# Layer norm's weight and bias folded into three evictions, its centring moved to GpSimd, and softmax sums taken over two banks at a time

## What is computed

```python
def layer0(z, ln_w, ln_b, Wq, Wk, Wv, Wg, bg, Wo, bo):      # H = 8 heads, C = 16
    mu = jnp.mean(z, axis=-1, keepdims=True)
    var = jnp.var(z, axis=-1, keepdims=True)
    zn = (z - mu) * jax.lax.rsqrt(var + EPS) * ln_w + ln_b
    q, k, v = zn @ Wq, zn @ Wk, zn @ Wv                     # each reshaped to heads
    g = jax.nn.sigmoid(zn @ Wg + bg)
    att = jnp.einsum('iabhc,jabhc->ijabh', q, k) * (1.0 / np.sqrt(C))
    att = jax.nn.softmax(att, axis=1)                       # over the 16 sequences j
    o = jnp.einsum('ijabh,jabhc->iabhc', att, v) * g
    return o.reshape(n, l, l, H * C) @ Wo + bo
x = x + layer0(_gn(x), ...)      # _gn: each sequence and channel normalised over the 32 x 32 positions
x = x + layer1(_gn(x), ...)
```

## Time and profile before

| | us |
|---|---|
| median of 3 runs (lowest, highest) | 340.28 (339.03, 341.97) |
| the profiled execution's own time | 342.18 |
| its span, first to last instruction | 340.2 |
| DVE / PE / ACT / POOL busy | 250.9 / 247.4 / 215.8 / 196.5 |
| first layer's strips, periods 0 to 9 | about 37 to 260 of the span |

### The profile page before, as it was taken

The page is one execution under the profiler, slowest core; times in us unless marked ns, Lnnn a source line. Parts: engine busy times, 40 slices in busy tenths (PEclk is TensorE's granted clock), DMA queues, the critical chain, the costliest instruction groups (busy, mean ns, idle before and its releaser), DMA issues.

```text
span 340.2 us, 7453 instructions
## 1 busy us (share of the span) xinstructions
PE 247.4 (73%) x2978; PEld 145.4 (43%) x2982; DVE 250.9 (74%) x463; ACT 215.8 (63%) x392; POOL 196.5 (58%) x172
## 2 busy tenths in 40 slices
...
DMA packets 34893, 19.66 MB, mean 58 GB/s; under 512 B 21228, under 2 KB 31788, under 8 KB 34860
## 3 DMA queue, kind: packets, MB, share of 16 engines
...
## 4 chain that ended last, share of the span: by engine, by line
DVE 40%; PE 40%; ACT 11%; issue 6%; DMA 1%; DVEq 0%; POOL 0%
PE PS L1128 35%; DVE nmax L899 5%; DVE t_sb L883 5%; DVE S_sb L903 5%; DVE og L876 4%; DVE gn_part L966 3%; DVE sums L827 3%; ACT PP L631 2%; PE PS L1197 2%; DVE Z L1115 2%; PE PS L1393 2%; DVE rden L845 1%; ACT t_sb L615 1%; DVE Z L1119 1%; ACT S_sb L621 1%
## 5 line engine op out<-in xcount | busy, mean ns | idle before, releaser
L1128 PE MATMUL PS<-znT,A_bd 128*128 128x512 f16 x192 | 47.0, 386 | 11.3 <-DVE t_sb L883 10.1
L428 POOL TENSOR_TENSOR S_sb<-S_sb,rden 128x512 f32<-128x512 f32 x32 | 35.5, 1133 | 27.6 <-DVE rden L845 27.6
L883 DVE TENSOR_TENSOR t_sb<-PS,t_sb 128x512 f16<-128x512 f32 x64 | 41.2, 684 | 9.2 <-ACT t_sb L615 8.7
L615 ACT CAST t_sb<-PS 128x512 f16<-128x512 f32 x64 | 36.6, 618 | 13.8 <-PE PS L1128 12.5
L621 ACT ACTIVATE S_sb<-S_sb 128x512 f32<-128x512 f32 x32 | 20.3, 634 | 31.7 <-DVE S_sb L903 31.7
L434 POOL TENSOR_TENSOR PP<-S_sb,PP 128x512 f16<-128x512 f32 x28 | 31.8, 1158 | 9.5 <-ACT PP L609 9.5
L1128 PE MATMUL PS<-zbd,t_sb 128*128 128x64 f16 x768 | 27.7, 196 | 12.9 <-DVE t_sb L883 12.2
L1128 PEld LDWEIGHTS PS<-zbd,t_sb 128*128 128x128 f16 x768 | 24.9, 100 | 24.0 <-DVE t_sb L883 16.5
L1128 PEld LDWEIGHTS PS<-znT,A_bd 128*128 128x128 f16 x192 | 16.7, 98 | 39.9 <-DVE t_sb L883 23.8
L411 POOL TENSOR_TENSOR ln_rs<-ln_ve,minus_half 128x16 f32<-128x16 f32 x7 | 20.4, 2914 | 23.0 <-DVE ln_ve L822 23.0
L601 ACT COPY u_sb<-PS 128x512 f32<-128x512 f32 x64 | 33.1, 642 | 0.2 <-PE PS L1128 0.2
...
## 6 DMA issues: line engine op xcount, KB each, us to landing
...
th<-k_dram SPq DMA_DIRECT2D x16, 128.0 KB, 2.7
...
PP<-u_sb SPq DMA_DIRECT2D x8, 128.0 KB, 2.4
```

The costliest lines, as they stand in the source:

```text
L428: nc.gpsimd.tensor_tensor(P, P, bcast(rden[:, 32 * k:32 * k + 32], 2, N), ALU.mult).then_inc(p_nrm, 1)
L615: nc.scalar.copy(t_sb[:, HI, :, h], bank_tg(h)[:, :].rearrange("p (q i) -> p q i", i=N)).then_inc(t_hi, 1)
L883: nc.vector.tensor_tensor(t_sb[:, LO, :, h], bank_tg(h)[:, :].rearrange("p (q i) -> p q i", i=N), t_sb[:, HI, :, h], ALU.subtract).then_in ...
L1128: return nc.tensor.matmul(o, l, r, start=start, stop=stop)
```

## The change

- ln_w and ln_b leave the stream of tokens. `pool_ln_back` loses its last two products, and strip 0 its two on DVE. zn is now only centred and scaled.
- In their place: A_bd carries ln_w on both sides (a per-partition scale `w_col4` in its ACT and DVE evictions, and `wkT` multiplied by `w_bc`); what ln_b adds to t is `t_bias`, added in ACT's cast of t and in DVE's difference (now scalar_tensor_tensor with a pointer); Wg is scaled by `w_col`, and bg_h takes in Wg^T ln_b; the u copies become activations with scale `w_col` and bias `b_col`. A part that is constant along the softmax drops out.
- The start-up gains one DMA (w_col and b_col for b_bc), two bias matmuls behind the transposes of Wq and Wk, one behind the products of A, and small DVE operations. PE's waits count them.
- Centring of strips 1 to 7 goes from DVE to POOL: DVE makes the sum and a scaled mean (`dve_ln_mean`, in a full period behind the first PT copy, in period 1 behind head 3), POOL subtracts (`pool_ln_centre`) in its queue behind the square of x and ahead of the normalisation of k = 2, 3. ACT's Square waits for POOL. Variance (`dve_ln_rstd`) moves behind `dve_stats`.
- `dve_sums` takes two banks in one reduce: k = 2, 3 behind both PT copies, k = 0, 1 behind the k = 2 subtraction.

```diff
         WPREP2 = 16 + 12 + 1 + 5 + 3
-        LZ, LV = 7, 4
+        LZ0, LZ, LV = 5, 6, 4
...
+        def pool_ln_centre(pool, j, par):
+            zf = zc[:, par].rearrange("p e b d -> p (e b) d")
+            pool.wait_ge(ln_v, LV * j + 2)
+            nc.gpsimd.tensor_tensor(zf, zf, bcast(ln_mu[:, par], 2, D), ALU.subtract).then_inc(ln_z, 1)
+
         def pool_ln_back(pool, j, par):
...
-            pool.wait_ge(ln_z, LZ * (j - 1) + 3)
+            pool.wait_ge(ln_z, LZ * (j - 1) + 4)
             nc.gpsimd.tensor_tensor(zf, zf, bcast(ln_rs[:, par], 2, D), ALU.mult).then_inc(ln_z, 1)
-            pool.wait_ge(ln_z, LZ * (j - 1) + 4)
-            nc.gpsimd.tensor_tensor(zf, zf, bcast(w_bc[:, :], 1, A2 * SB), ALU.mult).then_inc(ln_z, 1)
-            pool.wait_ge(ln_z, LZ * (j - 1) + 5)
-            nc.gpsimd.tensor_tensor(zf, zf, bcast(b_bc[:, :], 1, A2 * SB), ALU.add).then_inc(ln_z, 1)
...
             if stats:
                 pool_sqx(pool, j - 3)
+            if LN and not (j == 0):
+                pool_ln_centre(pool, j + 1, 1 - par)
             if tail:
                 pool_norm(pool, j - 1, (2, 3))
...
         def act_ln_square(act, j, par):
-            act.wait_ge(ln_v, LV * j + 2)
+            if j == 0:
+                act.wait_ge(ln_v, 2)
+            else:
+                act.wait_ge(ln_z, LZ * (j - 1) + 3)
...
-                    nc.scalar.copy(u_sb[:, :, 4 * k:4 * k + 4].rearrange("p h q i -> p q h i"),
-                                   bank_u(k)[:, :].rearrange("p (q h i) -> p q h i", q=4, h=H)).then_inc(u_ok, 1)
+                    nc.scalar.activation(u_sb[:, :, 4 * k:4 * k + 4].rearrange("p h q i -> p q h i"),
+                                         bank_u(k)[:, :].rearrange("p (q h i) -> p q h i", q=4, h=H), ACT.Identity,
+                                         bias=b_col[:, :], scale=w_col[:, :]).then_inc(u_ok, 1)
...
-                    nc.scalar.copy(t_sb[:, HI, :, h], bank_tg(h)[:, :].rearrange("p (q i) -> p q i", i=N)).then_inc(t_hi, 1)
+                    nc.scalar.activation(t_sb[:, HI, :, h], bank_tg(h)[:, :].rearrange("p (q i) -> p q i", i=N),
+                                         ACT.Identity, bias=t_bias[:, h:h + 1]).then_inc(t_hi, 1)
...
+        def dve_ln_mean(dve, j, par):
+            dve.wait_ge(ln_z, LZ * (j - 1) + 2)
+            nc.vector.tensor_reduce(ln_mu[:, par], zc[:, par].rearrange("p e b d -> p (e b) d"), op=ALU.add,
+                                    axis=AX.X).then_inc(ln_v, 1)
+            dve.wait_ge(ln_v, LV * j + 1)
+            nc.vector.tensor_scalar(ln_mu[:, par], ln_mu[:, par], 1.0 / D, None, ALU.mult).then_inc(ln_v, 1)
...
-        def dve_sums(dve, m, ks):
-            for k in ks:
-                dve.wait_ge(s_exp, 4 * m + k + 1)
-                nc.vector.tensor_reduce(sums[:, 32 * k:32 * k + 32], S_sb[:, 8 * k:8 * k + 8]
-                                        .rearrange("p q a n -> p (q a) n"), op=ALU.add, axis=AX.X).then_inc(p_sum, 1)
+        def dve_sums(dve, m, half):
+            dve.wait_ge(s_exp, 4 * m + 2 * half + 2)
+            nc.vector.tensor_reduce(sums[:, 64 * half:64 * half + 64], S_sb[:, 16 * half:16 * half + 16]
+                                    .rearrange("p q a n -> p (q a) n"), op=ALU.add, axis=AX.X).then_inc(p_sum, 1)
...
-                if tail:
-                    dve_sums(dve, m, (2 + i,))
+                if i == 0 and LN and not (j < 2):
+                    dve_ln_mean(dve, j + 1, 1 - par)
             if tail:
+                dve_sums(dve, m, 1)
                 dve_reciprocal(dve, m, 1)
-            if LN and not (j < 2):
-                dve_ln_centre(dve, j + 1, 1 - par)
-                dve_ln_rstd(dve, j + 1, 1 - par)
             if stats:
                 dve_stats(dve, s - 1)
+            if LN and not (j < 2):
+                dve_ln_rstd(dve, j + 1, 1 - par)
...
-                nc.vector.tensor_tensor(t_sb[:, LO, :, h], bank_tg(h)[:, :].rearrange("p (q i) -> p q i", i=N),
-                                        t_sb[:, HI, :, h], ALU.subtract).then_inc(t_lo, 1)
+                nc.vector.scalar_tensor_tensor(out=t_sb[:, LO, :, h],
+                                               in0=bank_tg(h)[:, :].rearrange("p (q i) -> p q i", i=N),
+                                               scalar=t_bias[:, h:h + 1], in1=t_sb[:, HI, :, h], op0=ALU.add,
+                                               op1=ALU.subtract).then_inc(t_lo, 1)
...
                     if h == 3:
-                        dve_ln_centre(dve, 2, 0)
+                        dve_ln_mean(dve, 2, 0)
...
-                if k in (1, 2):
-                    dve_sums(dve, j, (k - 1,))
                 if k == 2:
+                    dve_sums(dve, j, 0)
                     dve_reciprocal(dve, j, 0)
...
             dve.wait_ge(wT_mm, 1)
+            nc.vector.tensor_scalar(w_col4[:, :], w_col[:, :], 0.25, None, ALU.mult).then_inc(wprep, 1)
             nc.vector.tensor_copy(wqT[:, :, :], bcast(PS[4][:, 0:D], 1, A2)).then_inc(wprep, 1)
-            nc.vector.tensor_copy(wkT[:, :], PS[4][:, D:2 * D]).then_inc(wprep, 1)
+            nc.vector.tensor_tensor(wkT[:, :, :], bcast(PS[4][:, D:2 * D], 1, A2), bcast(w_bc[:, :], 1, A2),
+                                    ALU.mult).then_inc(wprep, 1)
+            nc.vector.tensor_copy(wb[:, :], PS[4][:, 2 * D:2 * D + 2]).then_inc(wprep, 1)
...
                                     bcast(headmask[:, :], 2, 128), ALU.mult).then_inc(wprep, 1)
+            nc.vector.tensor_scalar(qb[:, :], headmask[:, :], wb[:, 0:1], 0.25, ALU.mult, ALU.mult).then_inc(wprep, 1)
+            nc.vector.tensor_scalar(bg_h[:, :], bg_in[:, :], wb[:, 1:2], 0.5, ALU.add, ALU.mult).then_inc(wprep, 1)
...
-                    pe.wait_ge(wprep, 3)
+                    pe.wait_ge(wprep, 7)
                     for h in range(H):
-                        last = mm(PS[1][:, D * h:D * h + D], wqTm[:, h], wkT[:, :])
+                        mm(PS[1][:, D * h:D * h + D], wqTm[:, h], wkT[:, 0])
+                    last = mm(PS[1][:, 256:256 + H], wkT[:, :, :].rearrange("p e d -> p (e d)"), qb[:, :])
                     last.then_inc(wT_mm, 1)
```

More of the change, by code:

```diff
@@ L92, in build @@
         w_bc = sb("w_bc", [128, D])
-        b_bc = sb("b_bc", [128, D])
+        w_col = sb("w_col", [128, 1])
+        w_col4 = sb("w_col4", [128, 1])
+        b_col = sb("b_col", [128, 1])
+        wb = sb("wb", [128, 2])
+        qb = sb("qb", [128, H])
+        t_bias = sb("t_bias", [128, H])
         bo_col = sb("bo_col", [128, 1])
@@ L276, in wait_zn @@
             if j == 0:
-                engine.wait_ge(ln_0, LZ)
+                engine.wait_ge(ln_0, LZ0)
             else:
@@ L337, in _ @@
             sp.dma_start(w_bc[:, :], ln_w.partition_broadcast(128)).then_inc(wts_in, 16)
-            sp.dma_start(b_bc[:, :], ln_b.partition_broadcast(128)).then_inc(wts_in, 16)
+            for v, w in ((w_col, ln_w), (b_col, ln_b)):
+                sp.dma_start(v[:, :], w.unsqueeze(0).to_broadcast([A2, D]).unsqueeze(2)).then_inc(wts_in, 16)
             sp.dma_start(wo_in[:, :], Wo).then_inc(wts_in, 16)
@@ L528, in _ @@
             pool_clear2()
+            pool_ln_centre(pool, 1, 1)
             for j in range(3):
@@ L569, in act_ln_high @@
             if j == 0:
-                act.wait_ge(ln_0, 6)
+                act.wait_ge(ln_0, 4)
             else:
-                act.wait_ge(ln_z, LZ * (j - 1) + 6)
+                act.wait_ge(ln_z, LZ * (j - 1) + 5)
             if j >= 2:
@@ L714, in _ @@
                 rows = slice(D * g, D * g + D)
-                nc.scalar.mul(A_bd[rows, HI, :, g], PS[1][rows, 0:256].rearrange("p (h d) -> p h d", h=H),
-                              0.25).then_inc(wprep_a, 1)
+                nc.scalar.activation(A_bd[rows, HI, :, g], PS[1][rows, 0:256].rearrange("p (h d) -> p h d", h=H),
+                                     ACT.Identity, scale=w_col4[rows, :]).then_inc(wprep_a, 1)
             act.wait_ge(wts_in, WTS)
-            nc.scalar.mul(bg_h[:, :], bg_in[:, :], 0.5).then_inc(wprep_a, 1)
             act_ln_high(act, 0, 0, 0)
@@ L724, in _ @@
             act_ln_square(act, 1, 1)
-            nc.scalar.copy(Wg_s[:, HI], wg_in[:, :, :].rearrange("p h c -> p (h c)")).then_inc(wprep_a, 1)
+            nc.scalar.activation(Wg_s[:, HI], wg_in[:, :, :].rearrange("p h c -> p (h c)"), ACT.Identity,
+                                 scale=w_col[:, :]).then_inc(wprep_a, 1)
             for j in range(3):
@@ L841, in dve_reciprocal @@
         def dve_reciprocal(dve, m, half):
-            dve.wait_ge(p_sum, 4 * m + 2 * half + 2)
+            dve.wait_ge(p_sum, 2 * m + half + 1)
             if m >= 1:
@@ L847, in dve_gate_weights @@
         def dve_gate_weights(dve):
-            dve.wait_ge(wprep_a, 6)
-            nc.vector.tensor_tensor(Wg_s[:, LO], wg_in[:, :, :].rearrange("p h c -> p (h c)"), Wg_s[:, HI],
-                                    ALU.subtract).then_inc(wprep, 1)
+            dve.wait_ge(wprep_a, 5)
```

(13 more changed lines are left out.)

29 lines of the change are left out of this document (14 added, 15 removed).

## The result

| | before | after |
|---|---|---|
| median of 4 runs of each, in one measurement | 341.12 us | 359.37 us (358.94 to 360.27) |
| ratio, 95% interval | | 1.0562 [1.0518, 1.0607] |
| span of the profiled execution | 340.2 us | 357.5 us |
| DVE / PE / ACT / POOL busy | 250.9 / 247.4 / 215.8 / 196.5 | 245.0 / 258.0 / 232.0 / 183.8 |
| first scores of period 1 | 65.15 | 69.25 |

A forecast was written before the change was run, and what follows sets the result against it. Order and latency, not one engine's load, were taken to bound the kernel. Start-up and period 1 +5.0, loop +9.5 and end +1.5 sum to 16.0, giving 356 us; own range 353 to 359, full range 350 to 361.

The forecast's parts named there:

- rival 4: A longer stall in period 1 keeps PE's lower clock into strip 2's u and t matmuls: up to +4, 360; chance 0.13.
- u copies: Eight ACT copies a period, now with two pointers: +0.19 each, 1.52 a period, pe_o later by that less 0.1 slack.
- t casts and differences: One pointer each: ACT cast +0.10, DVE difference +0.05; heads 6 and 7 on the path add 0.2 together.
- Merged sums and centring in the loop: Full periods: merged DVE sums give -0.06; centring on POOL is all hidden, worth 0.
- Period 2: Period j = 2: +1.25, as PE's clock below full level while u is made leaves ACT about 0.5 to spare.
- Start-up and period 1: Up to period 1's scores, 70.2 and not 65.15: +5.0 together, bounds 1.8 and 6.
- The stall: Period 1: POOL's k = 2, 3 normalisation queues behind strip 2's centring, which waits for DVE's mean: about 3 us.
- rival 3: No stall in period 1, since what follows waited there for POOL's zn anyway: 353; chance 0.1.
- Period 8: Period before the last u period: DVE's weight splits hold the gate products until 239.41, no idle time before them: 0.
- Period 9: Last strip's u period: the eight u copies stand alone on the path, 8 x 0.19 = +1.5.

The follow-up runs named there:

- b_uptr: The kernel before with only its u copies made Identity activations with scale and bias pointers (ones and zeros): 348.94 us, ratio 1.0227 to before.
- u_bias: The kernel after with only the bias pointer on the u copies, the scale an immediate 1: 355.66 us, ratio 1.0416 to before.
- b_centre: The kernel before with only the centring of strips 1 to 7 moved to POOL, products with w and b kept: 353.16 us, ratio 1.036.
- b_sums: The kernel before with only the sums of P merged over two banks, placed as in after: 344.75 us, ratio 1.0122.
- both_orders: After, with POOL's k = 2, 3 normalisation ahead of centring in period 1 and DVE's mean behind the second PT copy in period 2: 354.55 us, ratio 1.0409.
- u_copy: The kernel after with its u copies plain COPY again, without scale and bias pointers: 350.91 us, ratio 1.0285 to before.

## Why the prediction was right, step by step

- **The number: close, in part by luck.** Forecast 356 on a median of 340.28, +16.0; measured 359.37 on 341.12, +18.25, and 17.3 in span. That is inside 350 to 361, but 0.4 above the forecast's own 353 to 359 and near rival 4's 360. Errors of both signs stand in it (below), and DVE's busy time fell by 5.9 us and not by about 3.
- **u copies: right in mechanism and size.** Forecast 0.67 from start to start and pe_o later by 1.42; measured 0.665 and 1.42, in after and, alone, in b_uptr. It was the row of the same function with the same operands that gave the price, and the absence of slack before pe_o that gave its place. The estimate from the Trainium skill (ScalarE: Activation LUTs, "What ACT_TABLE_LOAD costs") was 0.71; its 93 ns for a pointer agrees with the 0.72 us for eight between u_bias and after.
- **t casts and differences: right,** 0.38 forecast, 0.43 measured.
- **Merged sums and centring in the loop: the sum was right (-0.06), its reasons were not.** "Worth 0" and "-0.06" were told as properties of each edit; alone they cost 0.51 and 0.23 a period (b_centre, b_sums). The order between the PT copies was not looked at.
- **Period 2: wrong by 2.1 us.** "+1.25" moved the full period's costs into period 2 and did not ask whether POOL's front, which the mean now waits for in front of the second PT copy, is on time in the first full period. u starts 5.64 us behind the k = 3 subtraction where it was 3.21 in before, +2.43 that nobody forecast; from there on the period is 0.89 longer and not 1.25. In both_orders u starts 4.10 behind, so the mean's place is worth 1.54 at the start of u and 1.46 in the period. The other 0.89 stays open: in both_orders the transposes ahead of u begin 1.33 us behind the subtraction (0.96 in before), after a wait for POOL's zn, and ran at a granted clock of 0.50 (78 to 80 us); no run parts the two.
- **Start-up and period 1: the sum about right (5.33 for 5.0), its terms not.** The first scores of period 0 were 1.70 late (46.26 for 44.56) and not 1.95, the first t difference of period 1 1.36 and not 1.8. The stall was sized as 3 us; both_orders shows 2.3 (DVE idles 2.17 before p_low, so rival 3 falls), and the scores came 4.1 late instead of 5.0. From there to the k = 3 subtraction nothing was forecast, and it was 1.23 more (9.42 for 8.19). That is PE's clock, granted at 0.50 from 69 to 77 us. PE in after, in u_copy and in b_uptr:

```profile
69.25 2.74 PE L1151 MATMUL PS<-zbd,t_sb 128*128 128x64 f16 x48 [6.33 <-DVE t_sb L902]
71.92 1.46 PE L1151 MATMUL PS<-znT,Wg_s 32*128 32x512 f16 x6
```

```profile
70.83 1.10 PE L1150 MATMUL PS<-znT,Wg_s 32*128 32x512 f16 x6
71.86 0.87 PE L1150 MATMUL PS<-zbd,t_sb 128*128 128x64 f16 x24
```

```profile
64.76 2.74 PE L1133 MATMUL PS<-zbd,t_sb 128*128 128x64 f16 x48 [2.97 <-DVE t_sb L888]
67.43 1.46 PE L1133 MATMUL PS<-znT,Wg_s 32*128 32x512 f16 x6
```

  A piece of six gate matmuls takes 0.82 us at full level and 1.46 at the lower one; in after all of them up to 76 us take 1.46. Rival 4 says that the longer wait (6.33 us for 2.34) did that. But u_copy, with the same wait of 6.34, was back at full level by 71.9, and b_uptr, whose period 1 is that of before, with a wait of 2.97, was not by 73. So the return to full level moves by some us from one execution to the next, and these runs do not show that the change moved it. Whether the change caused the 1.23 us, and what the clock adds in period 2, stays open.
- **Period 8: wrong by 1.0.** The row said that no idle time stood before the gate products, and the forecast took the work ahead of them as of fixed length. It was stretched by POOL, whose start the change moved. In b_uptr, with the same pointers, the period is 1.98 us shorter than in before, in after only 1.01, since pe_o took 3.29 us and not 2.35 at the lower clock.
- **Period 9: right in the number, by luck in part.** 1.53 for 1.5. The eight copies took 5.47 us instead of 4.02, +1.45 as forecast. But they began 3.71 us behind the last line where before had 4.53, since before's transposes ran at a lower clock (0.57 from 244 to 246 us), and pe_o then took 3.22 us for 2.35, at 0.72 (268 to 272). In b_uptr, where pe_o took 2.35, the same copies lengthened the period by 0.62 only.

The errors of the sum, +0.3, +2.1, -0.2 and -1.0, with 0.1 elsewhere, make the 17.3 us of span out of the forecast's 16.0.
